# Graph layer, node blocks: the update bias moves from bf16 matmuls of its own into a fixed row 0 of each message window

## What is computed

```python
em = jnp.concatenate([x[src], x[dst]], axis=-1)
em = jax.nn.relu(layer_norm(em @ msg_w + msg_b, msg_g, msg_beta))
em = em * edge_weights[:, None]
msgs = jax.ops.segment_sum(em, dst, num_segments=num_nodes)
...
messages = msgs / (counts + 1e-08) * valid
gate = jax.nn.sigmoid(x @ gate_w + gate_b)
combined = jnp.concatenate([x, messages], axis=-1)
h_new = jax.nn.relu(layer_norm(combined @ upd_w + upd_b, upd_g, upd_beta))
return gate * h_new + (1.0 - gate) * x
```

## Time and profile before

| | |
|---|---|
| time, median of 3 runs (lowest, highest) | 630.3 us (629.31, 630.38) |
| the profiled execution: its time | 628.39 us |
| the profiled execution: its span, first to last instruction | 626.6 us |
| mean granted clock of PE | 0.971 of full speed |
| PE busy | 563.5 us (90%) |
| ACT busy | 535.7 us (85%) |
| DVE busy | 529.8 us (85%) |
| POOL busy | 387.1 us (62%) |
| moved by DMA | 118.44 MB, mean 189 GB/s |

### The profile page before, as it was taken

How to read it: one execution, slowest core, us unless ns; L and a number is a source line. 1 busy time by engine, 2 the same in 40 slices (tenths; PEclk the granted TensorE clock), 3 DMA queues, 4 the chain that set the end, 5 groups by cost and what they waited for, 6 DMA issues and landing times.

```text
span 626.6 us, 19668 instructions
## 1 busy us (share of the span) xinstructions
PE 563.5 (90%) x4796; PEld 541.1 (86%) x4796; DVE 529.8 (85%) x2428; ACT 535.7 (85%) x2500; POOL 387.1 (62%) x396
## 2 busy tenths in 40 slices
PE   1364799999999999999999999999999999999771
PEld 0343799999999999999999999999999999999761
DVE  3980158989989899998989989899899999989986
ACT  0021499999999999999999999999999999999883
POOL 1877777777777777777776767677676776300000
PEclk9976799999999999999999999999999999999996
DMA  4213577887878888787887877878787787756642
GB/s 112 64 48 88 136 200 206 208 234 202 231 215 216 221 209 225 204 221 217 217 230 189 226 213 208 230 195 221 210 214 219 204 229 197 208 156 171 182 117 67
DMA packets 199095, 118.44 MB, mean 189 GB/s; under 512 B 15053, under 2 KB 192662, under 8 KB 198934
## 3 DMA queue, kind: packets, MB, share of 16 engines
q1 hardware_dynamic: 184822, 91.95, 52.2%
q0 software_dynamic: 12544, 25.72, 17.2%
q10 hardware_dynamic: 1696, 0.40, 0.3%
HBM read 79.04 MB, written 38.97 MB: 188 GB/s over the span
## 4 chain that ended last, share of the span: by engine, by line
PE 87%; DVE 5%; ACT 5%; issue 2%; DMA 1%; SPq 0%; DVEq 0%; ACTq 0%
PE ps_u L761 14%; PE ps_u L763 13%; PE ps_z L742 9%; PE ps_z L729 7%; PE ps_z L727 7%; PE ps_t L778 7%; PE ps_x L750 6%; PE ps_h L785 6%; PE ps_u L703 3%; PE ps_xs L710 3%; PE ps_xs L736 3%; PE ps_xd L710 3%; PE ps_z L703 2%; DMA halo_i<-in_dst 1%; ACT squares L555 1%
## 5 line engine op out<-in xcount | busy, mean ns | idle before, releaser
L466 POOL DMA_INDIRECT pair_rows<-in_x,gather_idx x392 | 386.9, 987 | 151.5 <-issue 112.9
L761 PE MATMUL ps_u<-u_x_gate,xT 128*128 128x129 f32 x784 | 151.7, 275 | 0.0
L763 PE MATMUL ps_u<-window,onehot 128*128 128x128 f32 x784 | 151.2, 274 | 0.0
L761 PEld LDWEIGHTS ps_u<-u_x_gate,xT 128*128 128x128 f32 x784 | 118.7, 191 | 1.6
L763 PEld LDWEIGHTS ps_u<-window,onehot 128*128 128x128 f32 x784 | 119.0, 192 | 0.0
L588 ACT ACTIVATE un<-ps_u,u_rstd 128x128 f32<-128x128 f32 x392 | 112.0, 372 | 3.2
L1100 DVE TENSOR_SCALAR out_rows<-y,y_small,y_rstd 128x128 f32<-128x128 f32 x392 | 110.5, 355 | 4.6 <-ACT y_rstd L611 4.6
L1048 DVE SCALAR_TENSOR_TENSOR y<-ps_h,gate_small,x_rows 128x128 f32<-128x128 f32 x392 | 109.8, 342 | 1.2 <-PE ps_h L785 1.2
L555 ACT ACTIVATE squares<-ps_u 128x128 f32<-128x128 f32 x392 | 105.7, 288 | 3.0 <-PE ps_u L763 2.9
L555 ACT ACTIVATION_READ_ACCUMULATOR squares<-ps_u 128x1 f32 x392 | 85.6, 219 | 0.0
L1055 DVE BATCH_NORM_STATS2 y_stats<-y 128x6 f32<-128x128 f32 x392 | 84.6, 278 | 0.0
(11 more groups left out here) (133 smaller groups left out, 1119.2 us busy)
## 6 DMA issues: line engine op xcount, KB each, us to landing
window<-rows_scratch SPq DMA_DIRECT2D x196, 129.0 KB
x_rows<-in_x SPq DMA_DIRECT2D x98, 256.0 KB
out<-out_rows SPq DMA_DIRECT2D x98, 256.0 KB
rows_scratch<-msg_rows SPq DMA_DIRECT2D x49, 258.0 KB, 3.1
pair_rows<-in_x,gather_idx POOLq DMA_INDIRECT x392
const_in<-in_constants SPq DMA_DIRECT2D x1, 1037.0 KB, 5.1
rows_scratch<-pad_rows SPq DMA_DIRECT2D x5, 64.5 KB, 2.7
weights<-in_L_gnn_msg_w ACTq DMA_DIRECT2D x1, 128.0 KB, 5.3
```

The lines of the kernel that those rows point to most:

```text
L466: return nc.gpsimd.indirect_dma_start(rows[:, j * P:(j + 1) * P], None, x, bass.IndirectOffsetOnAxis(ap=offsets, axis=0))
L761: nc.tensor.matmul(u_tile(j, ROW), tile(xT[b], j), u_x_gate[:], start=False, stop=False, skip_group_check=True)
L763: last = nc.tensor.matmul(u_tile(j, P), tile(onehot[b], j), window[slot][:, j * ROW:j * ROW + P], start=False, stop=True, skip_group_check ...
```

## The change

The bias of the node blocks' update is put into row 0 of every window buffer, once, at the start. Row 0 of the one-hot matrix must then be all ones; that comes from a constant: the number in the last column of row 0 of the window is `ALWAYS` (2^60), and so is row 0 of the constants that it is compared with, and subtracting a node number from 2^60 leaves 2^60 in fp32. So the one-hot matmul adds the bias to each node. The window transfers now fill rows 1 to 127, with 127 rows for each tile where there were 128, and the threshold for the general branch goes from 128 to 127. The bias matmuls of `update` are gone, and the first matmul of x starts the accumulation. The gate's bias goes to the activation that reads the gates, as its bias operand. The general branch adds the bias to its own sums, and has its own row 0.

```diff
             def load_window(k, b, at):
                 slot = 2 * (k.c % 2) + b
                 for i in range(2):
-                    sp.dma_start(window[slot][:].rearrange("p (a i h) -> p i a h", i=2, h=ROW)[:, i],
+                    sp.dma_start(window[slot][1:P, :].rearrange("p (a i h) -> p i a h", i=2, h=ROW)[:, i],
                                  rows_dram[bass.ds(at + i * HALF, 2 * P), :].rearrange(
-                                     "(a p) h -> p a h", p=P)).then_inc(win_loaded[slot], 16)
+                                     "(a p) h -> p a h", p=P)[0:P - 1]).then_inc(win_loaded[slot], 16)
...
                 nc.scalar.activation(gate_exp[b][:].rearrange("p (a t) -> p a t", a=2).unsqueeze(3), u_gates,
-                                     ACT.Exp, scale=-1.0).then_inc(gate_exp_ready, 1)
+                                     ACT.Exp, bias=gate_bias[:], scale=-1.0).then_inc(gate_exp_ready, 1)
...
                 wait(pe, un_ready, k.at(4, 2 * b - 1 + a))
-                bias(ps_u[:, a * 512:a * 512 + 2 * ROW], upd_bias)
                 for j in (2 * a, 2 * a + 1):
-                    nc.tensor.matmul(u_tile(j, ROW), tile(xT[b], j), u_x_gate[:], start=False, stop=False,
+                    nc.tensor.matmul(u_tile(j, ROW), tile(xT[b], j), u_x_gate[:], start=True, stop=False,
                                      skip_group_check=True)
...
-            v.memset(bias_in[:, 0, P:ROW], 0.0)
+            for s in range(4):
+                v.memset(window[s][0:1, :].rearrange("p (j h) -> p j h", h=ROW)[:, :, P:ROW], ALWAYS)
...
+            for s in range(4):
+                v.tensor_copy(window[s][0:1, :].rearrange("p (j h) -> p j h", h=ROW)[:, :, 0:P],
+                              upd_bias[0:1].unsqueeze(1).to_broadcast([1, T, P]))
...
-            for j in range(T):
-                v.tensor_copy(msg_bias[:, j], bias_sum[:, 2, 0, 0:P])
-            for j in range(2):
-                last = v.tensor_copy(upd_bias[:, j], bias_sum[:, 2, 1])
-            last.then_inc(params_ready, 1)
+            v.tensor_copy(msg_bias[:], bias_sum[:, 2].unsqueeze(1).to_broadcast([P, T, P])).then_inc(params_ready, 1)
...
-                link(v.tensor_scalar(ends[:], ends[:], float(P), block_start[:], ALU.subtract, ALU.is_gt))
+                link(v.tensor_scalar(ends[:], ends[:], float(P - 1), block_start[:], ALU.subtract, ALU.is_gt))
...
                 v.scalar_tensor_tensor(tiles(onehot[b][:]), w[:, :, P:ROW].to_broadcast([P, T, P]),
-                                       tile_base[:, bass.ds(k.at(2 * T, b * T), 1)], tiles(iota_block),
+                                       block_base[:, bass.ds(k.at(2, b), 1)], tiles(iota_block),
                                        ALU.subtract, ALU.is_equal).then_inc(hot_ready, 1)
```

More of the change, by code:

```diff
@@ L21 @@
 FAR = float(1 << 20)
+ALWAYS = float(1 << 60)
 LN_EXP_SET = 6
@@ L51, in const_columns @@
 def const_columns(wt):
-    sizes = [P, T * P, 2 * T * P, 2 * T, 2, wt, 3, 1, T]
+    sizes = [P, P, T * P, 2 * T * P, 2 * T, 2, wt // T, 3, 1, T]
     return [sum(sizes[:i]) for i in range(len(sizes) + 1)]
@@ L77, in gnn_kernel @@
     MSG0 = PAD0 + -(-SPAN // P) * P
-    C_IDENT, C_IOTA, C_BOUND, C_BOUNDC, C_TBASE, C_TILE, C_PART, C_LIMIT, C_WIN, C_END = const_columns(WT)
+    C_IDENT, C_IOTA, C_PLACE, C_BOUND, C_BOUNDC, C_TBASE, C_BASE, C_PART, C_LIMIT, C_WIN, C_END = const_columns(WT)
     with ExitStack() as ctx:
@@ L96, in gnn_kernel @@
         iota_row = const_in[:, C_IOTA:C_IOTA + P]
-        iota_block = const_in[:, C_IOTA:C_IOTA + BN]
-        tile_base = const_in[:, C_TILE:C_TILE + WT]
+        iota_block = const_in[:, C_PLACE:C_PLACE + BN]
+        block_base = const_in[:, C_BASE:C_BASE + NB]
         ones = sb("ones", [P, P])
@@ L103, in gnn_kernel @@
         u_x_gate = sb("u_x_gate", [P, ROW])
-        msg_bias, upd_bias = sb("msg_bias", [P, T, P], BF16), sb("upd_bias", [P, 2, ROW], BF16)
+        msg_bias = sb("msg_bias", [P, T, P], BF16)
         columns = sb("columns", [P, 4])
+        gate_bias = sb("gate_bias", [P, 1])
         gather_idx = sb("gather_idx", [P, EG, 2 * T], I32)
@@ L173, in gnn_kernel @@
         w_mean = sb("w_mean", [P, 4])
-        bias_in = sb("bias_in", [P, 2, ROW])
+        bias_in = sb("bias_in", [P, 2, P])
         bias_mean = sb("bias_mean", [P, 2])
-        bias_left = sb("bias_left", [P, 3, 2, ROW])
-        bias_part = sb("bias_part", [P, 3, 2, ROW], BF16)
-        bias_sum = sb("bias_sum", [P, 3, 2, ROW])
+        upd_bias = sb("upd_bias", [P, P])
+        bias_left = sb("bias_left", [P, 3, P])
+        bias_part = sb("bias_part", [P, 3, P], BF16)
+        bias_sum = sb("bias_sum", [P, 3, P])
+        gate_b_in = sb("gate_b_in", [P, 1])
         halo_i = sb("halo_i", [P, 2, P + 2 * REACH], I32)
@@ L906, in _ @@
             dve.wait_ge(consts_loaded, 16)
-            v.tensor_reduce(bias_mean[:], bias_in[:, :, 0:P], AX.X, ALU.add)
+            v.tensor_reduce(bias_mean[:], bias_in[:], AX.X, ALU.add)
             link(v.tensor_reduce(w_mean[:], weights[:], AX.X, ALU.add))
@@ L910, in _ @@
             link(v.tensor_scalar(w_mean[:], w_mean[:], -1.0 / P, None, ALU.mult))
-            for i in range(2):
-                v.tensor_scalar(bias_left[:, 0, i, 0:P], bias_in[:, i, 0:P], bias_mean[:, i:i + 1], None, ALU.add)
-            v.tensor_copy(bias_left[:, 0, :, P:ROW], bias_in[:, :, P:ROW])
+            v.tensor_scalar(gate_bias[:], gate_b_in[:], -1.0, None, ALU.mult)
+            v.tensor_scalar(bias_left[:, 0], bias_in[:, 0], bias_mean[:, 0:1], None, ALU.add)
+            link(v.tensor_scalar(upd_bias[:], bias_in[:, 1], bias_mean[:, 1:2], None, ALU.add))
+            for s in range(4):
+                v.tensor_copy(window[s][0:1, :].rearrange("p (j h) -> p j h", h=ROW)[:, :, 0:P],
+                              upd_bias[0:1].unsqueeze(1).to_broadcast([1, T, P]))
             for i, centred in enumerate((w_src, w_dst, u_x_gate[:, 0:P], u_msg)):
@@ L1135, in sum_by_node @@
                 for j in range(T):
+                    last = v.tensor_scalar(iota_block[0:1, j * P:(j + 1) * P], iota_row[0:1, :], float(j * P), None,
+                                           ALU.add)
+                link(last)
+                for j in range(T):
                     v.tensor_scalar(block_nodes[:, j * P:(j + 1) * P], iota_row, float(j * P), None, ALU.add)
@@ L1159, in sum_by_node @@
                         sums_read, 1)
+                    dve.wait_ge(sums_read, q + 2)
+                    v.tensor_tensor(r[:, :, 0:P], r[:, :, 0:P], upd_bias[:].unsqueeze(1).to_broadcast([P, T, P]),
+                                    ALU.add)
                     v.tensor_copy(r[:, :, P:ROW], node_col[:].unsqueeze(2)).then_inc(sums_ready, 1)
@@ L1184, in constants @@
     rows = np.arange(P, dtype=np.float32)
-    places = np.arange(T * P, dtype=np.float32)
+    places = np.repeat(np.arange(T * P, dtype=np.float32)[None, :], P, 0)
+    places[0] = ALWAYS
     firsts = np.concatenate([min(q * T * P, n_nodes - T * P) + P * np.arange(T) for q in range(blocks)])
@@ L1194, in constants @@
     c[:, at[0]:at[1]] = np.eye(P)
-    c[:, at[1]:at[2]] = places[None, :]
-    c[:, at[2]:at[3]] = by_tile.reshape(1, -1)
-    c[:, at[3]:at[4]] = by_tile.T
-    c[:, at[4]] = rows * P
-    c[:, at[4] + 1] = (rows + P) * P
-    c[:, at[5]:at[6]] = firsts[None, :]
-    c[:, at[6]:at[7]] = np.eye(P)[:, :3]
-    c[:, at[7]] = limit
-    c[:, at[8]:at[9]] = HALF * np.arange(T)[None, :]
+    c[:, at[1]:at[2]] = rows[None, :]
+    c[:, at[2]:at[3]] = places
+    c[:, at[3]:at[4]] = by_tile.reshape(1, -1)
+    c[:, at[4]:at[5]] = by_tile.T
+    c[:, at[5]] = rows * P
+    c[:, at[5] + 1] = (rows + P) * P
+    c[:, at[6]:at[7]] = firsts[None, ::T]
+    c[:, at[7]:at[8]] = np.eye(P)[:, :3]
+    c[:, at[8]] = limit
+    c[:, at[9]:at[10]] = HALF * np.arange(T)[None, :]
     return c
```

4 lines of the change are left out of this document (2 added, 2 removed).

## The result

The changed kernel takes 1725.4 us (1722.99 to 1726.39), where the kernel before takes 629.8: a ratio of 2.739, 95% interval 2.734 to 2.744. The forecast was 1691 us with a range of 1560 to 1900.

A forecast was written before the change was run, and what follows sets the result against it. PE was taken to bound the kernel before; changed, windows in single file on one DMA engine: 62.7 before the loop, 1602 for 49 pairs of 32.7, 24 behind, 1.8 around, forecast 1691 us, bounds 1554 to 2044, 1560 to 1900 at 8 in 10.

The forecast's parts named there:

- What bounds the kernel before: Steady loop: PE is the bound, busy 480.00 of 480.00 us, with the DMAs off that path.
- The windows in single file: Window transfers of 127 partitions go through one DMA engine, all four of a pair on the same; 25.4 us a pair.
- The signs that it named: Profile after: one-hot waits many hundred us for windows, PE under 50% busy, mean rate near 70 GB/s, windows alone 21 GB/s.
- side by side: Rival 2: a pair's four window transfers each on a different engine, 6.4 us a transfer, about 850 us; 3 in 100.
- The sum: Loop time for a pair of blocks: windows 25.4, gathers 2.1 and turn-around 5.2 us, 32.7 us; 49 pairs, 1602 us.
- packets at 25.0 ns: Windows on the one engine: 1016 packets a pair at 25.0 ns each, 25.4 us.
- gathers and turn-around: Per pair: gathers interleaved on the engine, 2.1 us; from one pair's last window packet to the next pair's first, 5.2 us.
- DVE's side: Turn-around by last window's landing, one-hot, result instructions, out store and windows' issue: about 4.5 us, under the rows' 5.2.
- The terms outside the loop: Before the first window issue 62.7 us, after the last 24 us, around the span 1.8 us.
- a nanosecond taken from PE in the loop is worth a nanosecond: Loop: PE time removed shortens the kernel equally; 196 matmuls cost 21.6 us, gain about 20 us if nothing else happened.
- its 11 us of slack: Steady loop: ACT, busy 468.92 of 480 us, is 11 us from full, the limit on gains from PE.
- Rival 1: Window transfers of 127 partitions are spread all the same, so the kernel gets faster: 608 us, 600 to 620; 4 in 100.

The follow-up runs named there:

- run 7: Kernel before, bias matmuls kept, with windows of 112 rows from partition 0: 629.6 us, ratio 1.000.
- run 6: Kernel before without the node blocks' bias matmuls, ACT computing three sums of squares a block instead of four: 614.6 us; control with bias matmuls: 628.1 us.
- Run 1: Kernel before, bias matmuls kept, with window transfers of 127 partitions starting at partition 0: 1761.4 us, 2.798 times before.
- run 3: Changed kernel with windows of 124 rows, then of 122 rows, instead of 127: 728.0 us (ratio 1.157) and 1017.3 us (1.617).
- run 4: Changed kernel with one of the two transfers of each window kept at 127 partitions, the other at 112: 1072.3 us, ratio 1.704 to the kernel before.
- run 5: Kernel before without the bias matmuls in `update`, nothing in their place: 616.3 us, ratio 0.980.
- run 8: Changed kernel with each 127-partition window transfer cut into 112 and 15 partitions: 628.8 us, ratio 1.000 to the kernel before.
- run 9: Changed kernel with windows of 112 rows, each transfer cut into 64 and 48 partitions: 683.7 us, ratio 1.088 to the kernel before.

## Why the prediction was right

**What bounds the kernel before** was right: 13 us come from taking matmuls away, nothing from lighter windows (run 7), 1 us from a lighter ACT (run 6).

**The windows in single file** were right in mechanism, place and side. Run 1 shows the count of partitions as the whole cause, run 3 the steps between and, by the short packets, the number of engines; the stretch of 24.7 ns for a packet shows the rate. The signs that it named are there as well: 69 GB/s on average, PE busy for 45%. That the four transfers of a pair lie on the same engine is shown by run 4 and by the length of a pair: side by side they would take 6.4 us.

**The sum** was off by 34 us, 0.7 us a pair. Its terms: packets at 25.0 ns, where the line of run 4 gives 26.5, 1.5 us more for 1016; gathers and turn-around at 7.3 us, where the line gives 6.5. The two errors have opposite signs and partly cancel. That division is the line's; at the 24.7 ns of the stretch with windows alone the rest would be 8.3 us, so which term was mis-sized isn't settled. The turn-around was taken from the wrong side: the sum has 5.2 us for the rows' landing, and gave DVE's side 4.5. In the chain DVE's side decides, with 2.7 us from the second one-hot to the next issue and the start of the first packets on top, while SP waits for landed rows only 5.2 us in the whole run. Since the forecast had the two sides at nearly the same length, this did not show in the time. The terms outside the loop held: the first window is issued at 63.0 us, and behind the last one-hot, at 1699.7, there are 23 us to the end, where the sum had 62.7 and 24.

**A step that failed**, though not in the forecast's own sum: that a nanosecond taken from PE in the loop is worth a nanosecond. 21.6 us of matmuls gave 13 (run 5). The prediction read it off the full PE column and allowed ACT its 11 us of slack. But PE at 480.00 of 480.00 us also means that each wait shorter than a matmul's latency is invisible there. With the order fixed on all engines, 0.18 us of 0.44 a step turned into such waits: about half of it at `zn`, most of the rest at the first x matmul of a pair, where the cause is open, and little of it through ACT (run 6). Rival 1's price of 608 us was too low by that, and by the 4.5 us between the runs with and without a row 0 (620.8 and 616.3).

**Unforeseen**: SP's issue takes the length of the transfer (6050 ns). The prediction had it issue the four at 0.5 us each. That it cost little, since the packets of all that comes later would have had to queue on the same engine anyway, is an argument; no run has the single file without it.

## What to carry to other kernels

A DMA's partition count is a design number: one partition less, for a cause that has nothing to do with DMA, took 15 of 16 engines away from the transfer. Before slicing `[1:P]` off a tile that is loaded in a loop, look for a transfer of a prime count in the setup of the same trace (67 and 127 here): its rate tells the price, and a count with the divisor 16 keeps the gain (112 rows here, where 102 were needed). Cutting a transfer in two to keep both count and divisor costs the issuing queue's time; here the gain was gone with it (run 8), and another cut made the kernel 9% slower (run 9). How many engines a transfer uses can be counted before any timing, from the short packets that go with it.

## What the runs showed of the hardware

- The number of 4-byte packets goes by the engines that a transfer is spread over: against 128 partitions, 15 fewer a transfer with 127, 14 with 122, 12 with 124, none with 112, as if each engine in use had one.
- A transfer that goes through one DMA engine holds its issuing queue: 6.05 us at the median for one of 254 rows, 2.68 us with two engines, 0.52 with four, 0.36 with sixteen.
- The time to issue is not steady even for spread transfers of rows of 516 bytes: 590 ns for 64 partitions, 452 for 48, 318 for 112, 335 for 15.
- With 127 rows on partitions 0 to 126 the kernel (bias matmuls kept) takes 36 us longer than with them on 1 to 127 (bias matmuls gone), all of it between the issue of a pair's windows and their use.
- In a loop in which PE shows 100% busy, matmuls that were taken away gave 60% of their time (13 of 21.6 us).
